# Second attention: the shared PSUM banks of steps 2 to 11, three (4, 5, 6) in place of two (5, 6)

## The reference, cut to what matters

```
q = (x @ wq).reshape(B, L, NUM_HEADS, HEAD_DIM)
k_ctx = (h_ctx_kv @ wk_ctx).reshape(B, T, NUM_KV_HEADS, HEAD_DIM)
v_ctx = (h_ctx_kv @ wv_ctx).reshape(B, T, NUM_KV_HEADS, HEAD_DIM)
...
scores = jnp.einsum('blhd,bmhd->bhlm', q, k_full) * scale + mask
probs = jax.nn.softmax(scores, axis=-1)
out = jnp.einsum('bhlm,bmhd->blhd', probs, v_full)
return out.reshape(B, L, NUM_HEADS * HEAD_DIM) @ wo
```

## Time and profile before

| | us |
|---|---|
| time, median of 3 runs (2448.41 to 2448.85) | 2448.55 |
| the profiled execution, its own time | 2449.79 |
| its span | 2448.0 |
| PE busy | 2331.0 (95%) |
| DVE, ACT, POOL busy | 1740.0, 1739.6, 1327.3 |

### The profile page before, as it was taken

One profiled execution on the slowest core, in us unless ns is written; L12 is line 12 of the kernel. 1 busy time (PEld: TensorE's weight loads), 2 busy tenths in 40 slices (PEclk: granted clock), 3 DMA queues, 4 the chain that ended last, 5 costly groups with the idle time before them and its releaser, 6 DMA issues.

```text
span 2448.0 us, 50586 instructions
## 1 busy us (share of the span) xinstructions
PE 2331.0 (95%) x19062; PEld 1628.8 (67%) x19123; DVE 1740.0 (71%) x3346; ACT 1739.6 (71%) x3784; POOL 1327.3 (54%) x942
## 2 busy tenths in 40 slices
PE   7989999989999999999999999999799799999997
PEld 4677777767777777777777777777655444444444
DVE  5455767668988888888889888889411666666546
ACT  2235444458888888888888888888411688888897
POOL 1035555435666766666766667666500487878500
PEclk9989999999999999999999999999899999999999
DMA  5222322230001000010000100003200200000100
GB/s 189 70 85 84 91 86 81 78 138 13 6 18 49 18 18 1 18 49 18 18 3 17 49 18 18 18 1 138 89 28 11 72 25 16 23 17 22 55 3 18
DMA packets 42321, 108.36 MB, mean 44 GB/s; under 512 B 5060, under 2 KB 25928, under 8 KB 36936
## 3 DMA queue, kind: packets, MB, share of 16 engines
q1 hardware_dynamic: 40312, 102.28, 12.4%
q0 software_dynamic: 768, 2.10, 0.3%
q10 hardware_dynamic: 1008, 0.79, 0.1%
HBM read 99.78 MB, written 4.98 MB: 43 GB/s over the span
## 4 chain that ended last, share of the span: by engine, by line
PE 70%; DVE 11%; ACT 11%; issue 4%; POOL 2%; DMA 0%; another core or an unknown queue 0%; SPq 0%; ACTq 0%; DVEq 0%; POOLq 0%
PE psum L1670 6%; PE psum L2820 4%; PE psum L1765 4%; PE psum L1699 3%; PE psum L1715 3%; PE psum L1716 3%; PE psum L1718 3%; PE psum L2787 3%; PE psum L1700 3%; PE psum L1701 3%; PE psum L2184 3%; ACT l_p L2623 3%; PE psum L2753 3%; PE psum L513 2%; PE psum L515 2%
## 5 line engine op out<-in xcount | busy, mean ns | idle before, releaser
L1322 POOL TENSOR_TENSOR xn<-xn,l_p 128x512 f32<-128x512 f32 (+1 forms) x400 | 562.1, 1405 | 320.1 <-DVE l_plo L1490 308.0
L1490 DVE TENSOR_TENSOR l_plo<-l_p,l_phi 128x512 fp32r<-128x512 f32 (+1 forms) x464 | 440.4, 949 | 10.6 <-ACT l_p L1365 9.5
L2623 ACT ACTIVATE l_p<-psum 128x1024 f32<-128x1024 f32 x416 | 397.6, 1038 | 55.9 <-PE psum L2787 51.2
L1364 ACT ACTIVATE l_phi<-psum 128x512 fp32r<-128x512 f32 (+1 forms) x464 | 276.1, 595 | 100.8 <-PE psum L1701 60.1
L1540 DVE TENSOR_REDUCE l_mx<-psum 128x1 f32<-128x512 f32 (+2 forms) x512 | 303.7, 615 | 53.4 <-PE psum L1765 53.0
L1376 ACT ACTIVATE psum<-l_m 128x512 f32<-128x512 f32 x461 | 283.0, 616 | 7.9
L2598 POOL TENSOR_TENSOR l_rs<-l_ms,half_power 128x32 f32<-128x32 f32 x45 | 244.3, 5430 | 68.8 <-DVE l_ms L2648 58.7
L1365 ACT ACTIVATE l_p<-psum 128x512 f32<-128x512 f32 (+1 forms) x464 | 276.5, 596 | 0.0
L2820 PE MATMUL psum<-l_p,l_vs 64*32 64x256 f32 x6656 | 252.0, 378 | 6.9 <-POOL l_vs L2594 3.0
L1699 PE MATMUL psum<-l_qThi,l_kThi 128*128 128x512 f32 (+1 forms) x464 | 224.0, 483 | 0.9 <-ACT psum L1376 0.9
L1765 PE MATMUL psum<-l_kThi,l_qThi 128*128 128x512 f32 (+2 forms) x512 | 215.8, 450 | 6.8 <-ACT l_kThi L1457 2.3
(11 more groups left out here) (410 smaller groups left out, 5068.2 us busy)
## 6 DMA issues: line engine op xcount, KB each, us to landing
w_stage<-in_L_w_dram SPq DMA_DIRECT2D x76, 384.0 KB, 3.1
l_w<-in_L_w_qkv_dram SPq DMA_DIRECT2D x16, 1024.0 KB, 5.0
l_ct<-in_ctx_tiles_dram SPq DMA_DIRECT2D x52, 128.0 KB, 2.3
c_T<-in_ctx_T_dram SPq DMA_DIRECT2D x4, 1601.0 KB, 7.9
l_ctx<-in_ctx_T_dram SPq DMA_DIRECT2D x4, 1601.0 KB, 6.9
c_N<-in_ctx_dram SPq DMA_DIRECT2D x4, 1536.0 KB
s_wg<-in_L_gate_dram SPq DMA_DIRECT2D x4, 1024.0 KB, 10.8
s_wu<-in_L_up_dram SPq DMA_DIRECT2D x4, 1024.0 KB, 12.8
```

Of the source, the lines that this page charges most:

```text
L1322: g_.tensor_tensor(l2_acc[k][0:r, :], first[0:r, :], p_of(c)[0:r, :], ALU.add)\
L1364: act.activation(l2_phi[c % 3][0:r, :], src, ACT.Exp).then_inc(l2_e, 1)
L1490: v.tensor_tensor(l2_plo[c % 3][0:r, :], p_of(c)[0:r, :], l2_phi[c % 3][0:r, :].bitcast(F32), ALU.subtract)\
L2623: act.activation(l3_p[ring(odd, c)][:, :], psum[:, (c % 2) * 2 * BANK:(c % 2 + 1) * 2 * BANK], ACT.Exp, scale=float(D3) ** -0.5).then_inc( ...
```

## The change

The first 11 shared items of a turn's preparation (`THREE_TILL`: the projections of steps 2 to 11 and the first search, which stands in step 11) go round banks 4, 5 and 6. The 12 items after them, up to step 16, go round 5 and 6, beginning with 5 again. From step 17 on the list is as before. The prologue's list, for turn 0's preparation, is unchanged. The first item on bank 4 has a wait of its own: from n = 2 on it waits for the copy of bank 4 (`l2_o`).

```
-        BANKS = [5 + at % 2 for at in range(PAIR)] + [(3, 5, 6)[(at - PAIR) % 3] for at in range(PAIR, len(SHARED))]
+        THREE_TILL = sum(len(shared_at(c)) for c in range(TILE_END[0] - 1))
+        BANKS = [4 + at % 3 for at in range(THREE_TILL)] + [5 + (at - THREE_TILL) % 2 for at in range(THREE_TILL, PAIR)] + [(3, 5, 6)[(at - PAIR) % 3] for at in range(PAIR, len(SHARED))]
...
             elif of[own] == 3:
                 pe.wait_ge(l2_o, (n - 1) * TB + 1)
+            elif of[own] == 4 and n > 1:
+                pe.wait_ge(l2_o, (n - 1) * TB)
             else:
                 wait_freed(pe, sequence(n - 1)[0][last_in(n - 1, of[own])], n - 1)
```

## The result

| | us |
|---|---|
| before, median of 4 runs (2448.41 to 2450.96) | 2448.7 |
| changed, median of 4 runs (2465.75 to 2468.21) | 2466.1 |
| ratio, 95% interval | 1.0074 (1.0061 to 1.0087) |
| span of the profiled execution | 2463.9 |

The changed kernel is 17.4 us slower, which is 0.7%. Forecast were 2465.0, 2459 to 2470.

The account below looks back on a forecast made before the run. The prediction took TensorE's queue to bound the kernel. Its terms, 15.8 us lost at step 2, 3.2 regained at step 6 and 3.8 lost at step 12, sum to 16.4 us: forecast 2465.0 us, range 2459 to 2470.

Parts of the forecast that it names:

- What bounds: TensorE's queue sets the end: PE busy 1043.27 of 1050 us in turns 1 to 14, at clock 1.00.
- Steps 3 to 11: Projections there and the search of step 11 wait for nothing visible, so the third bank gains 0; bound 1.4 us.
- Step 2: Projection now on bank 4 waits 1.13 us for ScalarE's copy in 14 turns: 15.8 us lost.
- Step 6: The second tile's shift no longer waits 0.23 us for DVE's sum, in 14 turns: 3.2 us gained.
- Step 12: Projection waits for the reduction of step 11's search, 0.27 us later, in 15 turns; some 0.25 is left, 3.8 us.
- the prediction's own sign: In the trace after, the load of projection 12 waits some 0.5 us for the reduction instead of 0.24.
- Step 13: VectorE's subtraction moves with ScalarE's key copy, so the second search's wait takes back only the slack, about 0.03 us.
- Only the copy costs: Rival: the wait of step 13 swallows what step 12 loses; 12.6 us, 2461.2 us; chance 0.10.
- Nothing gives way: Rival: step 6 keeps its 0.23 us, step 12 costs all of its 0.27; 19.9 us, 2468.4 us; chance 0.12.
- the faster rival: Copy ends in time and projection 12's 0.24 us wait goes: 3.6 us gained, 2445.0 us; chance 0.03.

Follow-up runs that it names:

- e3: Changed kernel with its three banks in the order 5, 6, 4, so neither wait arises: 75.07 us a turn, ratio 1.0001 to the kernel before.
- e1: Kernel before, banks unchanged, plus one wait: the projection of step 2 also waits for ScalarE's copy of bank 4; 76.19 us a turn (12 turns), ratio 1.0072.
- e7: Changed kernel with ScalarE's copy of bank 4 one step earlier in its queue: 75.06 us a turn, ratio 0.9991 to the kernel before.
- e2: Kernel before with two banks, but the 12 items from the projection of step 12 on begin with bank 5 again: 75.06 us a turn, ratio 1.0009.
- e5: Changed kernel with GpSimd's multiplication of the second key group held until VectorE's 65-row subtraction of step 11 is done: 76.17 us a turn, ratio 1.0066.
- e6: Changed kernel with banks in the order 5, 6, 4 up to step 13, then 6, 5: 74.78 us a turn, ratio 0.9978 to the kernel before.
- e8: Changed kernel with banks in the order 5, 6, 4 up to step 12, then 6, 5: 75.05 us a turn, ratio 1.0004 to the kernel before.

## Why the prediction was right

*What bounds.* TensorE's queue, as said: the time moved by what its waits moved, and the clock stayed at 1.00 in the turns of the changed kernel.

*Steps 3 to 11, nothing.* Right, and shown by e3 alone: no wait appears, and a third bank there changes nothing within 0.1%.

*Step 2, 1.13 us in 14 turns.* Right: 1.13 at the loads, 1.10 at the matmuls, 14 waits. The latency of 0.05 us, read from another copy, held. e1 shows that the wait alone carries most of the loss, e7 that it hangs on the place of one ScalarE instruction.

*Step 6, 0.23 us back.* Right, 0.22; the margin of 0.04 us held: VectorE's sum did not move with TensorE (0.02 of 1.13).

*Step 12, 0.27 us.* The releaser was right and the size was off: 0.71, and a wait of 0.94 us where the prediction's own sign was some 0.5. The reduction behind the subtraction of the values is 0.25 to 0.27 later, as computed (e2 and e5 have a wait of 0.51), but the subtraction of step 11 had become 0.65 us longer. The prediction took durations from the old trace for instructions of two engines whose distance its own first term had changed.

*Step 13, 0.02 us back.* Mis-sized as well: 0.25. The prediction let VectorE's subtraction move with the key copy and keep its 0.90 us. The copy moved, but the subtraction no longer meets GpSimd's additions and takes 0.68.

The two misses are +0.44 and -0.23 a turn and nearly halve each other. The sum of 16.4 us stands against 17.4 measured; by turns, 14 times 1.36, it is 19.0 against 16.1 forecast for the same 14. The near hit of the total is in part luck: the turn grew by 1.36 where 1.15 was forecast, close to the 1.4 above which the prediction called itself wrong.

*The rivals.* "Only the copy costs" has its counterpart in e2 and e7 (step 12 gives back what it takes), but not in the changed kernel. "Nothing gives way" (19.9 us) is nearer to the 19.0 of the turns than the forecast is, but not for its reason: step 6 did give way, in every turn. The Trainium skill's rule ("Perfetto Trace Analysis", section "Matmuls") of rotating through more banks (the faster rival) is borne out only where waits were: e6. At the ten places where the change applied it, e3 shows it worth nothing.

## What to carry to other kernels

A further buffer helps only where the trace shows a wait for the last one; here that was at two of the 23 items, both just past the stretch that got the third bank. Taking away the first alone paid nothing (e8), both together paid 0.26 us a turn (e6); the second alone was not run. Before lending out a buffer, look up in the trace when its last reader ends against when the borrower starts: 1.08 us a turn could be read off beforehand, and using the buffer two steps later, or moving its reader one step up, costs nothing. And once a change shifts one engine against another, the durations of VectorE and GpSimd instructions that overlap in time can't be carried over from the old trace.

## What the runs showed of the hardware

VectorE's subtraction of two SBUF tensors (65 x 512) and GpSimd's multiplication (128 x 512) slow each other down in one direction only: the one that starts first keeps its time. They take 0.68 and 1.50 us when VectorE is 0.07 ahead, 1.33 and 1.04 when GpSimd is 0.25 ahead, 0.68 and 1.04 when they don't overlap (e5). The second one loses almost the whole overlap, 0.46 of 0.61 us in the first case and 0.65 of 0.79 in the second. Across the profiles of this study the longer times are 1.48 to 1.55 and 1.28 to 1.35 us. The Trainium skill, "SBUF — State Buffer", section "Who interferes with whom", says that a VectorE instruction with both inputs in SBUF contends with GpSimd's reads, and that the order of issue decides which of the two blocks. The runs agree with it, with the numbers above; the second one here loses some 0.15 us less than the overlap.

What I had not expected is how far such an order carries: a wait of 1.1 us at step 2 swapped the two engines at step 11, 25 us later, and did so in each of the 14 turns. Of the 1.13 us 0.89 reach VectorE's subtraction and 0.56 GpSimd's multiplication; why they lose unequal parts on the way was not followed up.

The wait can also cost more than its length: in one turn of e1, and in none of the others, the granted clock fell to 1.2 GHz behind it, for 1.6 us more.
